# Moving the adapter's units between the halves of a slot, with half of VectorE's reads put behind the next maxima

## The reference, cut to what matters

```python
# L0: x (8, 256, 160), ctx (8, 512, 96), 8 heads of 20
enc, ca = ctx[:, :508], ctx[:, 508:]
hs  = mha(x @ Wq, enc @ Wk, enc @ Wv)                  # 256 queries, 508 keys, 8 heads
q1  = einsum('btc,th->bch', ca, Wq_ca)[:, idx]         # 96 distinct rows, picked up to 256
hs1 = mha(q1, x, x)                                    # "token" branch
hs2 = mha(hs1 @ Wq, ca @ Wk_ca, ca @ Wv_ca)            # 4 keys
out = (hs + hs2) @ Wout + b_out + x
# L1: self-attention (20 heads of 64), cross-attention on ctx, gated feed-forward
```

## Time and profile before

| | us |
|---|---|
| median of 3 runs | 1473.61 (1472.61 to 1474.12) |
| the profiled execution's own time | 1475.56 |
| its span, from the first to the last instruction | 1473.8 |
| PE busy | 1360.7 (92%) |
| DVE busy | 1025.4 (70%) |
| ACT busy | 748.2 (51%) |
| POOL busy | 751.0 (51%) |
| mean granted TensorE clock | 0.929 |

### The profile page before, as it was taken

How to read it: one execution, slowest core, us unless ns; L and a number is a source line. 1 busy time by engine, 2 the same in 40 slices (tenths; PEclk the granted TensorE clock), 3 DMA queues, 4 the chain that set the end, 5 groups by cost and what they waited for, 6 DMA issues and landing times. The chain is left out here.

```text
span 1473.8 us, 38650 instructions
## 1 busy us (share of the span) xinstructions
PE 1360.7 (92%) x16460; PEld 1169.2 (79%) x16460; DVE 1025.4 (70%) x1902; ACT 748.2 (51%) x1356; POOL 751.0 (51%) x510
## 2 busy tenths in 40 slices
PE   4989899885999999999979999999999999999597
PEld 3777777764888898889857888888888888888587
DVE  4577777746777867786657777777777767665485
ACT  2356565552555554555425545454555555554264
POOL 2266777565434443444514545454555555455364
PEclk9588888967999999999978999999999999999699
DMA  5001110002000000000010000000010000000000
GB/s 131 12 10 46 47 32 2 2 2 65 2 2 2 2 2 2 2 2 2 2 39 7 2 7 2 7 2 7 2 45 2 2 2 2 2 2 2 12 15 23
DMA packets 31955, 20.33 MB, mean 14 GB/s; under 512 B 21414, under 2 KB 30314, under 8 KB 31786
## 3 DMA queue, kind: packets, MB, share of 16 engines
q1 hardware_dynamic: 31786, 17.86, 4.7%
HBM read 16.54 MB, written 1.31 MB: 12 GB/s over the span
## 5 line engine op out<-in xcount | busy, mean ns | idle before, releaser
L507 POOL TENSOR_TENSOR cross_probs_l<-cross_probs 128x1024 f16<-128x1024 f32 x160 | 303.6, 1897 | 276.5 <-ACT cross_probs L578 276.2
L578 ACT ACTIVATE cross_probs<-cross_score 128x1024 f32<-128x1024 f32 x160 | 163.9, 1024 | 249.9 <-PE cross_score L820 249.9
L507 POOL TENSOR_TENSOR self_probs_l<-self_probs 128x1024 f16<-128x1024 f32 x80 | 151.5, 1894 | 204.0 <-ACT self_probs L578 203.6
L675 DVE TENSOR_REDUCE cross_maxima<-cross_max 128x2 f32<-128x1024 f32 x160 | 194.6, 1216 | 7.4 <-PE cross_max L796 7.2
L1591 POOL TENSOR_TENSOR ad_probs_l<-ad_probs 128x1024 f16<-128x1024 f32 x64 | 120.8, 1893 | 97.7 <-ACT ad_probs L1668 97.0
L578 ACT ACTIVATE self_probs<-self_score 128x1024 f32<-128x1024 f32 x80 | 82.1, 1027 | 156.8 <-PE self_score L820 156.8
L840 PEld LDWEIGHTS cross_pv<-cross_v_h,cross_probs 128*128 128x128 bf16 x1280 | 116.6, 98 | 33.2 <-issue 28.2
L840 PE MATMUL cross_pv<-cross_v_h,cross_probs 128*128 128x65 bf16 x1280 | 135.3, 196 | 2.6 <-POOL cross_probs_l L507 2.6
L661 DVE TENSOR_TENSOR cross_qk_l<-cross_shared,cross_qk_h 128x256 fp32r<-128x256 f32 (+1 forms) x160 | 87.9, 556 | 69.0 <-ACT cross_qk_h L563 68.8
L841 PE MATMUL cross_pv<-cross_v_l,cross_probs 128*128 128x64 f16 x1280 | 133.9, 194 | 0.0
L842 PE MATMUL cross_pv<-cross_v_h,cross_probs_l 128*128 128x65 bf16 x1280 | 133.5, 193 | 0.0
(11 more groups left out here) (420 smaller groups left out, 4735.5 us busy)
## 6 DMA issues: line engine op xcount, KB each, us to landing
ad_ctx_rows<-in_ctx SPq DMA_DIRECT2D x8, 192.0 KB, 2.8
cross_ctx_rows<-in_ctx SPq DMA_DIRECT2D x8, 192.0 KB, 2.5
sw_raw<-in_L_xattn_wq SPq DMA_DIRECT2D x2, 640.0 KB, 6.2
sw_raw<-in_L_xattn_wk SPq DMA_DIRECT2D x2, 640.0 KB, 4.3
sw_raw<-in_L_xattn_wv SPq DMA_DIRECT2D x2, 640.0 KB, 3.8
cw_raw<-in_L_xattn_wq SPq DMA_DIRECT2D x2, 640.0 KB, 4.1
lr_raw<-in_L_xattn_w_ff SPq DMA_DIRECT2D x2, 640.0 KB
out<-x_rows SPq DMA_DIRECT2D x8, 160.0 KB, 1.9
```

The lines of the kernel that those rows point to most:

```text
L507: nc.gpsimd.tensor_tensor(probs_l[:, n % PR, :, :].rearrange("p j k -> p (j k)"), whole, whole.bitcast(BF16)[:, 1::2], ALU.subtract).then_ ...
L578: nc.scalar.activation(probs[:, n % PR, :, :].rearrange("p j k -> p (j k)"), score_bank[:, :], ACT.Exp, scale=SCALE).then_inc(exped, 1)
L675: nc.vector.reduce_max(out, scores, AX.X).then_inc(max_read, 1)
```

## The change

`items(g)` gets another order, and DVE's slot is written out anew.

- Each half now starts with its weigh groups: 0 and 1 in the first, 2 and 3 in the second (they were last in the first half, and all but last in the second).
- The first half then holds mt, e1, k, q, d1, s2; q and k come from the second half and change places. e1 is one slot later in the batch (offset 9, first half, instead of 8, second half).
- The second half holds all others: top first, then the set-up units, ot, v 1, xv, out 0, mq, qs, rows, ctx, x, out 1, v 0, d2, e3, qw. ctx is two slots earlier (offset -3 instead of -1), x one slot (-4 instead of -3).
- DVE in slot g: maxima of the first half; from g = 5 on the second-half units of slot g - 1; the first-half units of slot g; maxima of the second half; normalising; top; second softmax. In slots 0 to 3 and in the last one DVE reads the second-half units at the end of their own slot.
- `q_s` and `k_s` keep 5 pairs instead of 4; the waits on `qk_hi` and in `find_max` follow the swap of q and k.

```diff
-    KEPT = 4
+    KEPT = 5
+    DEFER = 4
...
+        def groups(step):
+            if (p := pair(g, WEIGH)) is not None:
+                out.extend((step, ("weigh", p, 2 * step + n)) for n in range(2))
+
+        groups(0)
         if (p := pair(g, MT)) is not None:
             out.append((0, ("mt", p)))
+        add(0, "e1", 9)
+        if (p := pair(g, 0)) is not None:
+            out += [(0, ("k", p)), (0, ("q", p))]
+        add(0, "d1", 7)
         add(0, "s2", 8)
-        add(0, "v", 4, 1)
-        add(0, "e3", 9)
-        add(0, "d1", 7)
-        if (b := batch(g, -1)):
-            out.append((0, ("ctx", b)))
-        add(0, "out", 10, 0)
-        add(0, "out", 10, 1)
-        if (p := pair(g, WEIGH)) is not None:
-            out += [(0, ("weigh", p, group)) for group in (0, 1)]
-        if (p := pair(g, 0)) is not None:
-            out += [(1, ("q", p)), (1, ("k", p))]
+        groups(1)
+        add(1, "top", 1, 0)
+        add(1, "top", 2, 1)
         if g < 4:
             out += [(1, key) for key in ([("w", 0), ("w", 1), ("ct",)], [("qk", n) for n in range(4)],
                                          [("g2",), ("vt",)], [("vo",)])[g]]
-        add(1, "top", 1, 0)
-        add(1, "top", 2, 1)
+        add(1, "ot", 9)
+        add(1, "v", 4, 1)
         add(1, "xv", 4)
-        if (b := batch(g, -3)):
-            out.append((1, ("x", b)))
-        add(1, "ot", 9)
-        add(1, "rows", 0)
+        add(1, "out", 10, 0)
         add(1, "mq", 3)
-        add(1, "d2", 7)
-        add(1, "v", 3, 0)
-        add(1, "e1", 8)
-        if (p := pair(g, WEIGH)) is not None:
-            out += [(1, ("weigh", p, group)) for group in (2, 3)]
         add(1, "qs", 4, 0)
         add(1, "qs", 5, 1)
+        add(1, "rows", 0)
+        if (b := batch(g, -3)):
+            out.append((1, ("ctx", b)))
+        if (b := batch(g, -4)):
+            out.append((1, ("x", b)))
+        add(1, "out", 10, 1)
+        add(1, "v", 3, 0)
+        add(1, "d2", 7)
+        add(1, "e3", 9)
         add(1, "qw", 6)
...
             def slot(g):
-                for step in range(ROUNDS):
...
+
+                p = pair(g, MAX)
+                if p is not None:
+                    maximum(p, 0)
+                if g > DEFER:
+                    units(g - 1, 1)
+                units(g, 0)
+                if p is not None:
+                    maximum(p, 1)
+                if (v := pair(g, WEIGH)) is not None:
+                    normalise(v)
+                for n in range(2):
+                    if (b := batch(g, 1 + n)) is not None:
+                        dve.wait_ge(top_filled, b * 2 + n + 1)
...
+                if (b := batch(g, 8)) is not None:
+                    second_softmax(b)
+                if g < DEFER or g == SLOTS - 1:
+                    units(g, 1)
...
-                    pe.wait_ge(emptied, order.read(("k", p)))
+                    pe.wait_ge(emptied, order.read(("q", p)))
```

More of the change, by code:

```diff
@@ L1728, in extra @@
                 if what == "q":
-                    dve.wait_ge(qk_hi, b * 2 + 1)
+                    dve.wait_ge(qk_hi, b * 2 + 2)
                     nc.vector.scalar_tensor_tensor(q_s[:, b % KEPT, :], q_t[:, :], const["low_q"], bank_[:, 0:SEQ],
@@ L1732, in extra @@
                 elif what == "k":
-                    dve.wait_ge(qk_hi, b * 2 + 2)
+                    dve.wait_ge(qk_hi, b * 2 + 1)
                     nc.vector.scalar_tensor_tensor(k_s[:, b % KEPT, 0:KEYS], k_t[:, :], const["low_k"], bank_[:, 0:KEYS],
@@ L1851, in split_output @@
                 nc.vector.tensor_tensor(wo_b[:, 1, :], raw_o[0:2 * HB, 1, :], wo_b[:, 0, :], ALU.subtract).then_inc(prepared, 1)
-            def slot(g):
-                for step in range(ROUNDS):
[L1855 to L1882, removed]
@@ new lines, in maximum, with normalise @@
+            def maximum(p, step):
+                dve.wait_ge(max_filled, p * ROUNDS + step + 1)
+                nc.vector.reduce_max(maxima[:, p % 2, step, :, 0], max_bank[:, :].rearrange("p (j k) -> p j k", j=2)[:, :, 0:KEYS],
+                                     AX.X).then_inc(max_read, 1)
+            def normalise(p):
+                dve.wait_ge(pv_done, p + 1)
+                groups = pv_bank[:, 0:4 * AV]
+                nc.vector.reciprocal(recip[:, :], groups.rearrange("p (g d) -> p g d", d=AV)[:, :, AD]).then_inc(recip_ready, 1)
+                dve.wait_ge(recip_ready, p + 1)
+                head = p % APAIRS * 2
+                out = attn[p // APAIRS % 2][:, :, head * AD:(head + 2) * AD].rearrange("p t (h d) -> p h t d", h=2)
+                nc.vector.tensor_tensor(out, groups.rearrange("p (h t d) -> p h t d", h=2, t=QT)[:, :, :, 0:AD],
+                                        recip[:, :].rearrange("p (h t) -> p h t", h=2)[:, :, :, None].to_broadcast([P, 2, QT, AD]),
+                                        ALU.mult).then_inc(attn_ready, 1)
@@ new lines, in units @@
+            def units(g, step):
+                for at, key in items(g):
+                    if at != step or key[0] in ("weigh", "mt", "d1", "e1", "qs", "xv", "s2", "top"):
+                        continue
+                    if key[0] in SETUP:
+                        set_up(key)
+                    else:
+                        extra(key)
+            def slot(g):
+                p = pair(g, MAX)
[11 more added lines that the diff above has]
+                        dve.wait_ge(top_filled, b * 2 + n + 1)
+                        nc.vector.reduce_max(top_q[:, CDIM + 4 * n:CDIM + 4 * n + 4],
+                                             max_bank[0:CDIM, :].rearrange("p (h k) -> p h k", h=4), AX.X).then_inc(top_read, 1)
+                if (b := batch(g, 8)) is not None:
+                    second_softmax(b)
+                if g < DEFER or g == SLOTS - 1:
+                    units(g, 1)
```

## The result

| | before | after |
|---|---|---|
| median of 4 runs, us | 1473.11 (1468.41 to 1474.12) | 1546.16 (1540.46 to 1550.18) |
| the profiled execution's own time | 1475.56 | 1550.06 |
| its span | 1473.8 | 1548.2 |
| mean granted clock | 0.929 | 0.875 |

The changed kernel is slower by 5.1%: the ratio is 1.0511 (1.0487 to 1.0534). The forecast was 1500 us, with a range of 1462 to 1535. The two profiled executions lie 74.4 us apart in span.

What follows compares the result with a forecast made beforehand. PE was taken to set the adapter's pace, at a 0.84 clock. Idle time of 8.4 us a round against 3.0 made a round 38.4 against 34.6; 3.8 times 7.25 rounds is +27 us, so 1500 us (1462 to 1535).

Steps and rivals of the forecast that it cites:

- the walk: One adapter slot on PE at the high clock: waits at mt, k and q idle it 1.4 to 1.5 us, cold 0.7.
- The tops: PE waits for DVE's late second maxima before a batch's two top maxima: 1.1 us each, 0.2 at the low clock.
- The wait ahead of L1974: PE's old gap ahead of d2, 1.24 us, 7 times, 7.9 us in all; predicted to go.
- the ends: Adapter's first slots (0 to 4) and last slots: taken as 0 each, between -2 and +2 and 0 to +2.
- the factor of 1.6: Estimate of how much longer a whole slot's PE work takes at the low clock than at the high one.
- A cold round: Four adapter slots (one batch) at the low clock in the new order: 27.1 x 1.6 + 4 x 0.7 + 0.4 = 46.6 us.
- today's 32%: Share of time at 1.2 GHz in the old kernel's steady adapter slots, kept for the new order.
- the same formula: Round time from warm (35.5 us) and cold (46.6) rounds by clock share: 1 / (0.68 / 35.5 + 0.32 / 46.6) = 38.4.
- rival B: Steady adapter slots mostly at the low clock: 75% cold gives 43.2 us a round, about 1536 us; chance 0.10.
- 231 to 241 us: Old kernel's trace: a stretch begun with PE fully busy, after which the clock rose again near 241.
- 34.6: Old kernel's us a round, taken for one that holds the work of a nearly full round.
- C: Rival: faster, as bank claims aren't late and the clock holds; 29.5 us a round, -37 us, about 1437; chance 0.20.

Runs made afterwards that it cites:

- e1: The changed kernel's new order, but DVE reads all second-half units at the end of their own slot: 1482.42 us, 1.0081 of before.
- e2: The changed kernel, but DVE reads the first of the three second-half units in its own slot and puts off the other two: 1518.03 us, 1.0319 of before.
- e8: The changed kernel, but DVE reads v 1 in its own slot, once a batch: 1531.25 us, 1.0402 of before.
- e6: As e1 (nothing put off), but DVE reads the second maxima ahead of k and q in all slots: 1469.53 us, 0.998 of before.
- e9: As e6, but the second maxima come ahead of k and q only in the two slots of a batch with a top: 1454.01 us, 0.9885.
- e12: The changed kernel, but DVE reads two of the three second-half units in their own slot and puts off only the third: 1480.99 us, 1.0068 of before.

## Why the prediction was wrong, by its own steps

**The direction and the waits held.** mt starts 2.57 us behind the slot's first maximum matmul (253.50 to 256.07) where the walk gave 2.4, the maxima are read at 1.77 (1.65), and idle time at mt and k is 1.15 + 0.28 (1.4 to 1.5). At the low clock it is shorter, as said: the waits at mt and k come to 17.0 us in the 24 steady slots, most of them cold, which is the 0.7 a slot of the walk. The tops wait 0.31 in this cold slot (0.2), 0.42 on average. The wait ahead of L1974 is gone, the ends are -0.8 and 1.6 (0 each, to 2), and the factor of 1.6 holds. A cold round was put at 46.6; the four kinds of slot take 13.7, 10.2, 11.9 and 11.9, together 47.6.

**What failed: how much of the time is at the low clock.** The forecast kept today's 32%, and its own range went to 50%; it is 76%. With 76% the same formula, 1 / (0.24 / 35.5 + 0.76 / 46.6), gives 43.3, 4.9 a round more than the 38.4 of the forecast: 35 us over 7.25 rounds. This is rival B, to which I gave 0.10, and its "for" was the right reason: a gap in each slot leaves no stretch like 231 to 241 us. Its "against" (cold work fills the gaps) is true of their length, 0.5 to 1.1 us at mt, and with such gaps the share was 76%. The rows that I had, a fall behind one gap of 1.24 us and none behind another loss of that size ("about half the time"), spoke of falls alone; what matters as much is how long the clock then stays low, and in before that ended in a stretch free of gaps, which the change takes away. How many or how long the gaps must be for that is open, as e1 and e2 show with the same idle time at 0.79 and 0.66. With the gaps filled the share is 30 to 36% and a round 38.6 to 39.7, beside the forecast's 38.4 with 32%: the forecast was about the time of a kernel that kept its clock.

**What was missing: v.** "A weigh group waits for v's low part" is not in the walk; I treated the put-off reads as banks to be emptied and forgot that one of them is data for the next slot's first matmuls. The wait is 10.1 us in seven, 1.4 a round, 10 us over the adapter. 43.3 + 1.4 = 44.7 a round, against 44.9 measured. Undoing it gave 15, but through the clock: PE's idle time moved to other waits (e8), so the 1.4 is the length of the wait and not its worth.

**The sum again.** 44.7 less 34.6 is 10.1 a round, times 7.25: 73 us, against 73.6 in these slots. The 76% and the 1.4 in it are measured, so this shows that the other terms fit together, and isn't a forecast. Rival B as priced (1536) lacked only v. The chance of slower (0.64) was on the right side; C failed where it says it would, as the claim at mt is later than the weigh pair covers.

## What to carry to other kernels

A read that frees a bank of a short ring must not be put behind something that the producing engine's next slot itself starts: count the places of the ring to see whose claim it holds, and ask of each moved unit whether its output is also data for the first work of the next slot. Only the last of three such reads could be moved here at no cost in time. When a change turns one gap in four slots into one in each, price it with the clock that the gaps leave behind: here idle time was 14 us and the clock 46 of the 60. A few useless matmuls in the gap (never beyond its length) are the quick test of that, with the same matmuls at another place beside them to see what added work does anyway. Where DVE's order makes one unit or another wait, it can be chosen per slot, as the two slots with a top show.

## What the runs showed of the hardware

Work that is added to PE can make it finish earlier: four more matmuls in each of 30 slots, 96 of them in the steady ones, and the time falls by 2.1% (1546.16 to 1514.14, ratios of 1.0511 and 1.0303 to the kernel before).

Not expected either: a small DVE instruction that lasts 5 us. In e6 (and once each in e1, e9 and e12, with 4.7) the product of the second softmax, 96 by 32 elements with both inputs in SBUF, took 5.05 us; the median of the eight in e6 is 362 ns.

```profile
166.32 5.05 DVE L1797 TENSOR_TENSOR ad_p2n<-ad_p,ad_rec 96x32 f32<-96x32 f32 x1
```

POOL beside it:

```profile
165.97 0.87 POOL L1589 TENSOR_TENSOR x_rows<-x_rows,ad_raw_bo 128x320 f32<-128x320 f32 x1
166.80 3.75 POOL L1594 TENSOR_TENSOR ad_probs_l<-ad_probs 128x1024 f16<-128x1024 f32 x2
170.50 0.77 POOL L1598 TENSOR_TENSOR ad_xv_l<-x_rows,ad_xv_h 128x320 f16<-128x320 f32 x1
171.22 1.48 POOL L1603 TENSOR_TENSOR ad_probs_ql<-ad_probs_q 128x768 f16<-128x768 f32 x1
```

It ends at 171.37, 0.1 us after an unbroken run of four POOL instructions (the second row is two). The Trainium skill, in "SBUF — State Buffer" (Who interferes with whom), says that a DVE instruction with two inputs in SBUF contends with a GpSimd instruction that reads SBUF. The rows fit that, and go further: DVE didn't get its turn between POOL's instructions. It makes v's read late, and so the single wait of 4.2 to 4.8 us at the weigh groups in e1, e6, e9 and e12. The cause is read from the two timelines, and no run took POOL's work away to test it.
